# Indirect DMAs of GpSimd wait for their own slot's scores instead of the preceding slot's maxima

## What is computed

```python
xn = _layernorm(x)
x = x + causal_attention(xn, 16 heads of 8) + fp4_ffn(xn, 352)
xn = _layernorm(x)
x = x + attention_with_distance_decay(xn, 16 heads of 8) + mixture_of_experts(xn)
```

```python
scores = jax.nn.softmax(xf @ Wg, axis=-1)
top_w, top_idx = jax.lax.top_k(scores, TOP_K)          # TOP_K = 2
hdn = jax.nn.gelu(jnp.einsum('td,edh->eth', xf, W1) + b1[:, None, :], approximate=False)
y_e = jnp.einsum('eth,ehd->etd', hdn, W2) + b2[:, None, :]
y = jnp.einsum('etd,te->td', y_e, combine)
```

## Time and profile before

| | us |
|---|---|
| median of the timed executions | 1180.3 (1180.26, 1180.3, 1183.22) |
| the profiled execution | 1174.48 |
| its span, first to last instruction | 1172.6 |

### The profile page before, as it was taken

The page is one execution under the profiler, slowest core; times in us unless marked ns, Lnnn a source line. Parts: engine busy times, 40 slices in busy tenths (PEclk is TensorE's granted clock), DMA queues, the critical chain, the costliest instruction groups (busy, mean ns, idle before and its releaser), DMA issues.

```text
span 1172.6 us, 29516 instructions
## 1 busy us (share of the span) xinstructions
PE 881.4 (75%) x12187; PEld 432.8 (37%) x12187; DVE 847.7 (72%) x1425; ACT 666.2 (57%) x1015; POOL 353.0 (30%) x417
## 2 busy tenths in 40 slices
PE   0577776887887887886677678777788798788875
PEld 0355553343343344343222223332433344344322
DVE  6799947778888888787878856556576567566735
ACT  3233331665556555543466466547667777677786
POOL 3233242212312312203030264453333423523230
PEclk9999987899999999887789889988999989899999
DMA  8700052445235225133212141154265344544125
GB/s 136 236 19 18 25 120 62 104 87 128 63 70 128 60 73 129 52 87 83 50 50 56 45 107 44 46 148 106 64 167 132 94 128 121 139 116 105 53 85 159
DMA packets 115383, 108.30 MB, mean 92 GB/s; under 512 B 14113, under 2 KB 108210, under 8 KB 114866
## 3 DMA queue, kind: packets, MB, share of 16 engines
q1 hardware_dynamic: 108146, 94.85, 32.3%
q0 software_dynamic: 7104, 11.57, 3.7%
HBM read 64.65 MB, written 48.33 MB: 96 GB/s over the span
## 4 chain that ended last, share of the span: by engine, by line
PE 39%; DVE 19%; ACT 13%; issue 10%; another core or an unknown queue 2%; POOL 1%; DMA 1%; SPq 0%; ACTq 0%; DVEq 0%; POOLq 0%
PE a_psO L1206 12%; DVE a_maxes L1430 9%; ACT a_Pt L1277 8%; PE a_psS L1188 5%; PE a_psS L1168 5%; PE a_psS L1053 3%; PE a_psM L1147 2%; PE a_psM L1081 1%; ACT a_Pt L1273 1%; PE a_psM L1153 1%; PE a_psM L1224 1%; DVE xn L1465 1%; ACT parts L1248 1%; PE a_psM L1109 1%
## 5 line engine op out<-in xcount | busy, mean ns | idle before, releaser
L1430 DVE TENSOR_REDUCE a_maxes<-a_psS 128x2 f32<-128x1024 f32 (+3 forms) x432 | 507.0, 1183 | 191.0 <-PE a_psS L1053 168.9
L1277 ACT ACTIVATE a_Pt<-a_psS,alpha 128x512 f32<-128x512 f32 x512 | 315.3, 698 | 114.8 <-PE a_psS L1053 96.3
L1168 PE MATMUL a_psS<-K,Q 60*64 60x512 bf16 (+3 forms) x2048 | 183.4, 371 | 96.1 <-ACT a_Pt L1277 42.1
L1206 PE MATMUL a_psO<-a_Pt,V 128*32 128x512 f32 (+3 forms) x2048 | 241.6, 561 | 14.9 <-ACT a_Pt L1277 11.7
L1188 PE MATMUL a_psS<-Q,K 63*64 63x512 bf16 (+3 forms) x2048 | 182.1, 372 | 37.6 <-DVE a_maxes L1430 30.5
L1273 ACT ACTIVATE a_Pt<-a_psS 128x1024 f32<-128x1024 f32 (+1 forms) x176 | 162.5, 944 | 83.7 <-PE a_psS L1053 83.1
L313 POOL TENSOR_TENSOR qkf<-qkf,parts 128x512 f32<-128x512 f32 x32 | 37.0, 1157 | 326.4 <-ACT parts L1248 323.8
L1168 PEld LDWEIGHTS a_psS<-K,Q 60*64 60x64 bf16 x2048 | 61.6, 113 | 173.4 <-ACT a_Pt L1277 61.7
L1188 PEld LDWEIGHTS a_psS<-Q,K 63*64 63x64 bf16 x2048 | 59.2, 108 | 175.6 <-DVE a_maxes L1430 76.3
L1053 PE MATMUL a_psS<-dist,eye 64*64 64x64 bf16 x2048 | 106.8, 199 | 0.0
L1570 POOL DMA_INDIRECT y<-spare,r_sent_id x64 | 61.6, 962 | 120.0 <-ACT spare L1309 60.4
(11 more groups left out here) (231 smaller groups left out, 1278.5 us busy)
## 6 DMA issues: line engine op xcount, KB each, us to landing
stack<-parts SPq DMA_DIRECT2D x192, 128.0 KB
expert_w<-in_expert_w SPq DMA_DIRECT2D x96, 128.5 KB
Q<-stack SPq DMA_DIRECT2D x64, 192.0 KB
K<-stack SPq DMA_DIRECT2D x64, 192.0 KB
xs<-in_c_no_token SPq DMA_DIRECT2D x24, 258.0 KB, 5.9
slots_flat<-xs SPq DMA_DIRECT2D x24, 258.0 KB
xnT<-xnT_dram SPq DMA_DIRECT2D x16, 256.0 KB
slots_flat<-y SPq DMA_DIRECT2D x16, 256.0 KB, 4.5
```

The source lines that it names most:

```text
L1168: pe.matmul(banks[HEAD_ROWS * hf:HEAD_ROWS * (hf + 1), b, x * w:(x + 1) * w], Q[rows, k % 4, q, at:at + HEAD_ROWS], K[rows, k % 4, q, 0:w] ...
L1206: m = pe.matmul(psO[32 * j:32 * (j + 1), q0:T], V[:, (k - 2) // 2 % 2, kt, r, j, :], Pt[:, (nB.at(k) + unit) % RING, h % 2, x // 2 * w:(x ...
L1277: m = act.activation(Pt[:, u % RING, b, :], scores[:, b, :], ACT.Exp, bias=0.0, scale=n.alpha[:, h:h + 1])
L1430: dve.tensor_reduce(maxes[:, k % 2, i, :, heads[0] // 2:heads[0] // 2 + pairs], src, AX, ALU.max, negate=True).then_inc(a_free, 1)
```

## The change

Only POOL's program changes, in three places. The semaphore that paces an indirect DMA becomes the one that PE raises for the slot's own scores: `a_ready` at `nA.at(k) + arg + 1` for the 151 DMAs that go with an A, and `b_ready` at `nB.at(k) + arg + 1` for the 9 that go with a B of step 32.

```diff
                                 set_ids(index // TILES)
                                 pool.wait_ge(slots_ready, index // TILES + 1)
-                            pool.wait_ge(a_free, nA.at(k) + arg)
+                            pool.wait_ge(a_ready, nA.at(k) + arg + 1)
                             scatter(index)
                         elif what == "EY":
                             to_send.extend((k, arg, i) for i in range(GROUP))
                         elif to_send and what == "A":
-                            pool.wait_ge(a_free, nA.at(k) + arg)
+                            pool.wait_ge(a_ready, nA.at(k) + arg + 1)
                             send_result(*to_send.pop(0))
                         elif to_send and what == "B" and k == HALVES:
-                            pool.wait_ge(p_ready, nB.at(k) + arg)
+                            pool.wait_ge(b_ready, nB.at(k) + arg + 1)
                             send_result(*to_send.pop(0))
```

## The result

The changed kernel takes **1161.06 us** (median of 4 executions, 1156.2 to 1163.14). The kernel before, run beside it, takes 1181.12 us (4 executions, 1180.26 to 1183.22). The ratio is 0.984, with a 95% interval of 0.9802 to 0.9877. That is 20 us faster by the medians and 19 us by the ratio, where 11 were forecast.

The account below looks back on a forecast made before the run. No engine exceeds 75% busy; handovers bound the kernel, PE's signals coming late while an indirect DMA is issued. Terms -9 - 5 + 4 - 1 = -11 us took 1180.3 to 1169.3 us; forecast as told 1162 to 1176, range 1156 to 1185.

Parts of the forecast that it names:

- Item 1: POOL's program: 160 waits are exchanged, no instruction added or removed, other work keeps its order; worth nothing.
- Item 2: Each paced DMA starts 0.28 us after its own slot's scores; 70 units instead of 118 end in the window, mostly late.
- Item 3: Delays behind single DMAs on the chain, some 13 us in stretched L1053 pieces: two thirds go, minus 9 us (0 to 13).
- Item 4: Five runs of closely spaced DMAs, 22.7 us of freezes: each loses its last DMA or so, minus 5 us (0 to 10).
- Item 5: PE's side jobs beside sends now end in the window; 10 of about 56 pay 0.4 us, plus 4 us (0 to 17).
- the slower rival: PE's side jobs in the window (28 of 56) each cost 0.6 us on the path: 1192 us, or 1184 to 1190; chance 0.16.
- Item 6: Granted clock: shorter freezes may save one stretch at the lower level, minus 1 us (plus 3 to minus 6).
- Item 7: Tail: DVE idles 10.00 us before its last steps, so earlier or later last sends are worth 0.
- Conserved delay: A DMA holds back whatever PE signals next, wherever it starts; only part of the runs' gain: 1177 to 1182 us; chance 0.14.
- The DMA held behind the reduction: DVE's 1.23 us maxima keep POOL from its DMA, so the window meets the next scores: 1176 to 1181 us; chance 0.04.
- More than the sum: The DMA runs break up altogether, half of 22.7 us goes, and the clock follows: 1152 to 1158 us; chance 0.10.

Follow-up runs that it names:

- e7: Changed kernel with all 160 indirect DMAs replaced by plain DMAs to consecutive places, so rows are not sorted or returned; 1134.15 us, 0.9629 of the kernel before.
- e2: Changed kernel, but each indirect DMA waits for PE's scores of the slot ahead instead of its own slot; 1169.41 us, 0.9901 of the kernel before.
- f1: Changed kernel with an unused POOL sum of 160 columns ahead of each pacing wait, to space the DMAs; 1154.72 us, 0.9792 of the kernel before.
- f3: Changed kernel with an unused POOL sum of 48 columns ahead of each pacing wait; 1165.66 us, 0.9844 of the kernel before.
- f4: Changed kernel with an unused POOL sum of 320 columns ahead of each pacing wait; 1169.78 us, 0.9937 of the kernel before.
- f2: Kernel before, with its old waits, plus an unused POOL sum of 160 columns ahead of each pacing wait; 1148.98 us, 0.9777 of the kernel before.
- e1: Changed kernel, but each indirect DMA waits for the maxima (step 32: exponentials) of its own slot; 1176.33 us, 0.9978 of the kernel before.
- e6: Changed kernel with an unused POOL sum of 160 columns between each wait and its indirect DMA; 1149.35 us, 0.9772 of the kernel before.
- e5: Changed kernel with an unused POOL sum of 512 columns between each wait and its indirect DMA; 1196.41 us, 1.0137 of the kernel before.

## Why the prediction was right, and where its sizes were off

The measured 1161.06 us lies inside the stated range of 1156 to 1185 us, but just below the 1162 to 1176 of the forecast as told: the direction and the mechanism were right, the size was too small.

**The mechanism** (PE's signals late behind an indirect DMA) holds, and e7 shows it without an argument from the timeline: the same program with plain DMAs has none. Of the words "while an indirect DMA is being issued", the form of the DMA matters and its issue time does not. What inside the chip holds the signals back is open.

**Item 1**, nothing for POOL's own work: right. Its busy time is 352.8 us.

**Item 2.** The starts moved as told: DMA 0.30 us behind its scores, DVE at 0.05. The count did not follow. 98 units end in the 0.3 to 1.3 us window, against 118 before, where I had laid 70 over the old timeline; with the delays gone the slots moved together. Yet only 58 signals are late in place of 114, because many of those 98 end at the edge: 29 in its last tenth, 1.2 to 1.3 us after a start, of which 18 are not late at all, 7 by about 0.1 us and 4 by 0.3 to 1.0 us. Before, 8 ended there. Over all late units the lag adds up to 46 us in place of 101. That most would fall late in the window, as the prediction had it, was the part that carried the gain.

**Item 3**, -9 us for single DMAs: the stretched pieces on the chain lost 9.5 us, and the wait of 1.81 us in step 25, which the prediction counted with them, is gone too. e2 gives 11 us for the phase. Right, and slightly low.

**Item 4**, -5 us for the runs: the term that was mis-sized. The long pieces lost 9.4 us, at the upper end of the 0 to 10 given. I had let each run lose one DMA, and each of the five did lose exactly one. What was wrong is the price of 1.27 us for it: the piece of step 26 vanished whole, three others lost 1.2 to 2.1 us each, and the first grew by 0.8 us. A run's freeze does not go by the number of its DMAs. f1, f3 and f4 show that their distance counts, at an unchanged number. A likely reason, not tested by itself: a signal held by one DMA comes 1.3 to 1.7 us after that DMA's start, and 1.27 us apart the next DMA has begun by then. The change leaves the distance in the remaining runs at 1.27 us, so the distance does not explain the 9.4 us; why these pieces shrank unevenly is open.

**Item 5**, +4 us for side jobs: did not appear. More of PE's other groups end in the window (112 against 90 before), but the expert steps are 11.4 us shorter (261.0 against 272.4) and within 3.2 us of e7, which has no lag at all. I had let 10 side jobs pay 0.4 us each on the path; the one shown above, 1.10 us into its DMA, paid nothing, and of all side jobs from 655 to 1136 us, counted as the score units are, 12 of 146 are late in after and 12 of 144 in before. With these steps shorter, the slower rival falls.

**Item 6**, the clock, -1 us: 53.0 us at the lower level after step 20 against 63.4. It goes the right way and is small. From kernel to kernel this time varies between 28.7 and 89.8 us, and single profiles do not show how much of that is cause and how much chance.

**Item 7**, the tail: nothing was seen there.

Set against the forecast's terms, the chain gives -11.3 for item 3 (9.5 and the 1.81 us), -9.4 for item 4, and -2.1 for the piece at 797.52 us, which no item had: -22.8 us, of which the span shows 17.2 and the medians 20. The other 5.6 us went into work elsewhere on the chain, which I have not assigned. So the forecast's 9 us of error cannot be split exactly; items 4 (4.4 us too small) and 5 (4 us that did not come) are its two largest parts.

**The other rivals.** Conserved delay: excluded by e2, which only moves the DMAs and whose interval ends at 0.9939. The DMA held behind the reduction: DVE's maxima took 1.23 us at 943.08 with a DMA begun at 943.32 inside them, and that DMA took 0.96 us. "More than the sum" gave 1152 to 1158 us and half of the runs' time gone. The measured 1161 us lies between it and the forecast; of its terms the one for the runs (-11) was nearer than mine.

**Left open:** whether the new phase and the wider spacing add up. f1 and f2 were to show it and did not, since the sum shifts the phase in both. A spacing in the scatters alone, with after's sends, would combine 134 to 137 us with 261.0 us; it was not tried.

## What to carry to other kernels

An indirect DMA of GpSimd can cost other engines more than it costs its own: look at what TensorE signals within 1.3 us of its start, and at runs of such DMAs 1.3 us apart. When a chain holds long pieces that no instruction explains, lay them over the DMA starts; spreading a run out, even by idle work, may be worth more than moving single ones. And a delay that is put in as an experiment changes distances as well as moments, so read from the trace what it has done before taking its time as an answer.

## What the runs showed of the hardware

- PE's signal to DVE, ACT or POOL mostly comes late when PE finishes 0.3 to 1.3 us after the start of an indirect DMA (94 of 118 such units in before, 51 of 98 in after; in after 12 of 17 that ended 1.0 to 1.2 us behind a start, and 2 of 32 that ended 1.4 to 1.6 us behind one). It mostly arrives about 0.6 us (0.59 in e1) or 1.3 to 1.7 us after that start (86 of 114 late units in before). Behind plain DMAs of the same queue none of 94 such units was late.
- In runs of three to six indirect DMAs 1.27 us apart the signals mostly stay away for 3 to 5 us (chain pieces of 2.84 to 5.26 us). At 1.75 to 2.02 us they come through between: of PE's score signals 0 to 5 are over 1 us late (f1, f2, e6, f4), at 1.56 us 23 (f3). At 2.34 us, with POOL short of time, they are 9 (e5).
- An indirect DMA of 128 rows keeps POOL for 0.96 us, a plain one for 0.54 us.
- A DMA behind a POOL wait that PE releases starts 0.30 us after the scores, but at least 0.78 us after them when a POOL sum stands ahead of the wait, also where that sum had ended long before (11 us in one case of f1). Behind the end of DVE's maxima it is 0.28 us in before and 0.76 us in f2, which has the sum.
- Some rises of semaphores are missing from a trace while indirect DMAs are being issued (13 of after's 71 late records belong to units whose reader had already started), and none is missing in e7.
